# Two-layer transformer stack on one core: routed experts on gathered row blocks instead of on all rows

## The reference

```python
x = x + attn_a(layernorm(x))      # 16 heads of width 8 over 256 positions, relative position bias
x = x + ffn(layernorm(x))
x = x + attn_b(layernorm(x))      # attends over the 32 batch entries, for each of 256 positions and 16 heads
x = x + ffn(layernorm(x))

# ffn: one shared expert for every row, and the best 2 of 7 routed experts
out = expert(x, sg, su, sd)                       # silu(x @ g.T) * (x @ u.T), then @ d.T, inner width 352
probs = softmax(x @ wr.T + rb);  scores, idx = top_k(probs, 2);  scores /= scores.sum()
out += sum over e of w[:, e] * expert(x, rg[e], ru[e], rd[e])     # w is 0 but for the two chosen
```

## Time and profile before

| | before |
|---|---|
| median of three runs | 3308.56 us |
| span of the profiled execution | 3301.8 us |
| TensorE busy | 3036.2 us, 92% |
| VectorE busy | 2308.3 us, 70% |
| ScalarE busy | 1813.0 us, 55% |
| GpSimd busy | 1737.1 us, 53% |
| mean granted TensorE clock | 0.928 |
| moved by transfers | 139.94 MB, 42 GB/s |

### The profile page before, as it was taken

One profiled execution on the slowest core, in us unless ns is written; L12 is line 12 of the kernel. 1 busy time (PEld: TensorE's weight loads), 2 busy tenths in 40 slices (PEclk: granted clock), 3 DMA queues, 4 the chain that ended last, 5 costly groups with the idle time before them and its releaser, 6 DMA issues.

```text
span 3301.8 us, 87667 instructions
## 1 busy us (share of the span) xinstructions
PE 3036.2 (92%) x29986; PEld 2069.9 (63%) x29986; DVE 2308.3 (70%) x6980; ACT 1813.0 (55%) x3489; POOL 1737.1 (53%) x1382
## 2 busy tenths in 40 slices
PE   7899999999999999999999789999999999999998
PEld 4567666666666666666666456666666666666665
DVE  4568776767787677767767656766767667676667
ACT  5568666756676677667765334443434444444443
POOL 4145445544544464446444336665656666666664
PEclk7799999989999999999989779998989999998999
DMA  3011111111111111111111111111111111111111
GB/s 112 20 33 42 36 36 33 40 35 33 39 39 33 36 36 39 36 33 36 41 31 36 43 34 47 50 47 44 49 45 47 44 50 50 47 50 47 50 47 49
DMA packets 105967, 139.94 MB, mean 42 GB/s; under 512 B 13121, under 2 KB 51265, under 8 KB 105585
## 3 DMA queue, kind: packets, MB, share of 16 engines
q1 hardware_dynamic: 87408, 126.18, 12.8%
q10 hardware_dynamic: 18176, 8.92, 1.1%
HBM read 126.11 MB, written 8.95 MB: 41 GB/s over the span
## 4 chain that ended last, share of the span: by engine, by line
PE 81%; DVE 8%; issue 5%; ACT 1%; DMA 1%; POOL 1%; ACTq 0%; DVEq 0%; SPq 0%; POOLq 0%
PE bank_E L1236 13%; PE bank_E L1238 9%; PE bank_E L1237 9%; PE bank_T L1166 7%; PE bank_Y L1236 6%; PE bank_S L1157 6%; PE bank_Y L1238 4%; PE bank_Y L1237 4%; PE bank_O L1177 4%; PE bank_S L1129 3%; PE bank_O L1218 3%; PE bank_S L1138 3%; PE bank_S L1139 2%; PE bank_S L1201 1%; DVE xn L909 1%
## 5 line engine op out<-in xcount | busy, mean ns | idle before, releaser
L593 POOL TENSOR_TENSOR hid_lo<-work,hid_hi 128x512 fp32r<-128x512 f32 x660 | 841.1, 1287 | 766.4 <-ACT hid_hi L836 757.2
L725 POOL TENSOR_TENSOR work<-work 128x512 f32<-128x512 f32 x640 | 827.6, 1300 | 482.2 <-DVE work L1075 362.2
L829 ACT ACTIVATE work<-bank_E 128x512 f32<-128x512 f32 x704 | 420.1, 597 | 466.7 <-PE bank_E L1238 462.0
L1075 DVE TENSOR_TENSOR work<-work,bank_E 128x512 f32<-128x512 f32 x704 | 479.8, 683 | 170.8 <-PE bank_E L1238 75.1
L836 ACT ACTIVATE hid_hi<-work 128x512 fp32r<-128x512 f32 x704 | 441.5, 630 | 282.1 <-POOL work L725 181.9
L1068 DVE SCALAR_TENSOR_TENSOR work<-work,bank_E 128x512 f32<-128x512 f32 x704 | 480.2, 682 | 148.0 <-ACT work L829 146.2
L981 DVE CUSTOM_DVE_ANT_0 z<-bank_S,big 128x256 f32<-128x256 f32 x1024 | 390.4, 421 | 200.7 <-PE bank_T L1166 147.5
L787 ACT ACTIVATE z<-z,nm 128x256 f32<-128x256 f32 x1024 | 457.4, 501 | 40.9 <-DVE nm L981 39.0
L583 ACT COPY probT<-bank_T 128x512 f32<-128x512 f32 x512 | 296.5, 579 | 105.2 <-PE bank_T L1166 102.4
L1236 PE MATMUL bank_Y<-hid_hi,wd_hi 128*128 128x512 f32 x704 | 327.7, 465 | 24.8 <-POOL hid_lo L593 19.5
L1236 PE MATMUL bank_E<-xh,wu_hi 128*128 128x512 f32 x704 | 330.1, 469 | 1.0 <-DVE work L1068 0.8
(11 more groups left out here) (125 smaller groups left out, 4345.9 us busy)
## 6 DMA issues: line engine op xcount, KB each, us to landing
work<-wts_dram SPq DMA_DIRECT2D x224, 256.0 KB, 3.2
work<-wts_dram SPq DMA_DIRECT2D x128, 192.0 KB, 2.7
work<-wts_dram SPq DMA_DIRECT2D x128, 128.0 KB, 2.8
work<-wts_dram SPq DMA_DIRECT2D x128, 64.0 KB, 2.5
xin<-in_x SPq DMA_DIRECT2D x16, 256.0 KB, 2.8
x<-work ACTq DMA_DIRECT2D x16, 256.0 KB, 2.5
xin<-x SPq DMA_DIRECT2D x64, 64.0 KB, 1.9
out_x<-work ACTq DMA_DIRECT2D x64, 64.0 KB, 1.7
```

What stands on the lines that cost most here:

```text
L593: eng.tensor_tensor(hid_lo[:, n % CUT_RING, :], hid[:, n % H_RING, :], hid_hi[:, n % CUT_RING, :].bitcast(F32), ALU.subtract).then_inc(hl_ ...
L725: pool.tensor_tensor(h, h, weight[:, k % WB_RING, :], ALU.mult).then_inc(weighed, 1)
L829: act.activation(th[:, n % 2, :], product_bank(2 * n)[:, :], ACT.Tanh, scale=0.5).then_inc(th_ready, 1)
L1075: dve.tensor_tensor(hid[:, n % H_RING, :], th[:, n % 2, :], product_bank(2 * n + 1)[:, :], ALU.mult).then_inc(h_ready, 1)
```

## The change

The program is rewritten around the same mathematics:

- The passes keep the shared expert alone: 3 tiles (128, 128 and 96 columns). Its gate and up products keep three fp32r matmuls, its down product is one plain f32 matmul a tile, and the low part for it goes.
- A pass ranks its rows by chosen expert (two triangular products, "rank") and scatters each row twice, with its weight and its row number, into the region of its expert in memory (sent), by eight indexed transfers of 128 rows from GpSimd ("scat").
- After all 16 passes of a half, VectorE makes a table of which block of 512 rows belongs to which expert; 38 blocks (BLOCKS) are always run. SP reads the table, pads the regions, and fetches rows (six ahead) and weights (three ahead). A block is transposed, goes through its expert's three tiles, is transposed back and weighted, and GpSimd adds its rows into x2 or x3 by four indexed adding transfers, each block's after those of the block before have landed.
- The routed weights are cut into high and low parts once at the start and kept in memory (w_split).
- In A the selector matmuls go: 32 transfers a pass lay q and k out. In B 16 transfers put k of each head into a zeroed tile kw, and the scores are matmuls over 128 rows and 512 columns in four column tiles; the transposes are made on TensorE, and v is laid out by position so that the product with it is 16 matmuls of 36 columns for each quarter of a pass.
- The planner now lays out all 16 passes of a half at once, two passes ahead with the load and one with the projections, with new costs; there is no loop in the code any more. Rings are deeper (z 6, probT 8), and bank T is two banks. Stores go from the ACT queue to SP's; half B ends in x3 and is copied to the output.

The core of the diff:

```diff
-Z_RING = 4
-PT_RING = 5
+BLOCKS = 2 * ROWS // CHUNK + ROUTED - 1
+Z_RING, NM_RING, PT_RING = 6, 8, 8
+ZB_RING, PB_RING = 4, 2
+ROW_RING, WEIGHT_RING = 6, 3
...
+                        for k in range(4):
+                            src = (qk_hi, qk_lo)[(k // 2, k % 2)[n]][32 * j:32 * j + 32, n, :]
+                            dst = qx[32 * j + 8 * k:32 * j + 8 * k + 8, s, n, :, :]
+                            sp.dma_start(dst, src).then_inc(spread_landed[2 * s + n], 16)
...
+                    for h in range(HEADS):
+                        sp.dma_start(kw[8 * h:8 * h + 8, h, :], k_b[8 * h:8 * h + 8, :]).then_inc(kw_landed, 16)
...
+            def pad(half):
+                sp.wait_ge(table_ready, half + 1)
+                for e in range(ROUTED):
+                    r = sp.value_load(table[0:1, 2 * BLOCKS + e:2 * BLOCKS + e + 1], min_val=0,
+                                      max_val=EXPERTS * CAP - CHUNK)
+                    sp.dma_start(sent[bass.ds(r, CHUNK), :].rearrange("(t p) c -> p t c", p=P), padding[:, :, :]
+                                 ).then_inc(padded, 16)
...
+                    for k in range(2):
+                        for t in range(TOK):
+                            pool.indirect_dma_start(
+                                out=sent[:, :], out_offset=bass.IndirectOffsetOnAxis(
+                                    ap=target[:, s, k, t:t + 1].bitcast(U32), axis=0),
+                                in_=xs[:, s, k, t, :], in_offset=None).then_inc(sent_out[s], 16)
...
+                for b in range(half * BLOCKS, (half + 1) * BLOCKS):
+                    pool.wait_ge(emptied["T1"], use("E", b, "back"))
+                    after(pool, added, 64 * b)
+                    for t in range(TOK):
+                        pool.indirect_dma_start(
+                            out=dst[:, :], out_offset=bass.IndirectOffsetOnAxis(
+                                ap=xr[:, b % ROW_RING, t, D + 1:RW].bitcast(U32), axis=0),
+                            in_=yo[:, b % 2, t, :], in_offset=None, compute_op=ALU.add).then_inc(added, 16)
...
+            pool.memset(kw, 0.0).then_inc(kw_ready, 1)
...
+                    for j in range(4):
+                        lo = n * P + 32 * j
+                        last = pe.matmul(bank[name][32 * j:32 * j + 32, :], q_b[:, p % 2, lo:lo + 32],
+                                         kw[:, :, lo:lo + 32], start=True, stop=True, tile_position=(0, 32 * j))
...
+                    last = pe.matmul(bank["Y"][:, :], shared_d[0:size, n, :], hid[0:size, n, :], start=n == 0, stop=n == NT - 1)
...
+            def blocks(half):
+                first, last = half * BLOCKS, (half + 1) * BLOCKS
+                block_turn(first)
+                for b in range(first, last):
+                    block_products(b, 0)
+                    if b > first:
+                        block_down(b - 1, 2)
+                    if b + 1 < last:
+                        block_turn(b + 1)
+                    block_products(b, 1)
+                    block_down(b, 0)
+                    if b > first:
+                        block_back(b - 1)
+                    block_products(b, 2)
+                    block_down(b, 1)
+                block_down(last - 1, 2)
+                block_back(last - 1)
...
+            run("pe", "A", head, attention, tail)
+            blocks(0)
+            run("pe", "B", head, attention, tail)
+            blocks(1)
```

More of the change, by code:

```diff
@@ L121, in weight_loads @@
[L121 to L144, removed]
-WORK = {
[L149 to L156, removed]
-    "logits": {"pe": 1.6, "dve": 0.3}, "route": {"dve": 0.6, "act": 0.1},
-    "wturn": {"pe": 0.5, "dve": 0.6, "act": 0.1, "sync": 4.0}, "gate": {"pe": 0.65, "act": 0.5, "dve": 0.6},
-    "up": {"pe": 0.65, "dve": 0.6}, "weigh": {"pool": 1.25}, "cut": {"act": 0.55, "pool": 1.25, "dve": 0.6},
-    "down": {"pe": 0.65}, "sum": {"act": 0.5}, "end": {"pe": 0.5, "dve": 0.6, "act": 0.1},
-}
@@ new lines, in attention_uses @@
+def attention_uses(kind, p):
+    if kind == "A":
+        out = [(f"S{u % 2}", p, "scores", u) for u in range(UNITS)] + [(f"T{u % 2}", p, "probs", u) for u in range(UNITS)]
+        for n in range(MIXES):
+            out += [("O", p, "mix", n), ("O", p, "context", n)]
+        return out
+    out = [(f"S{t % 2}", p, "scores", t) for t in range(TOK)] + [(f"T{t % 2}", p, "probs", t) for t in range(TOK)]
+    return out + [("O", p, "mix", t) for t in range(TOK)] + [("O", p, "bturn", 0), ("O", p, "bout", 0)]
@@ new lines, with emptier @@
+LISTS = bank_uses()
+PLACE = {key: (name, k) for name, keys in LISTS.items() for k, key in enumerate(keys)}
+EMPTIES = {
+    "A": {"turn1": "act", "q": "act", "k": "act", "v": "dve", "scores": "dve", "probs": "act", "mix": "dve",
+          "context": "dve", "turn2": "act", "logits": "dve", "rank": "dve", "down": "act", "end": "dve",
+          "gate": "dve", "up": "dve"},
+}
+EMPTIES["B"] = EMPTIES["A"] | {"bturn": "act", "bout": "dve"}
+def emptier(kind, p, step, n):
+    if step == "down":
+        return ("act", p, "sum", 0)
+    return (EMPTIES[kind][step], p, step, n)
@@ L295, in steps_experts @@
[L295 to L313 removed]
+            return free_bank(kind, p, step, n)
@@ L314, in takes_part @@
+        return [("pe", p, "end", 0), ("sync", p - 2, "store", 0)]
+    if step == "store":
+        return [("dve", p, "end", 0)]
+HEAD_STEPS = ("load", "keep", "norm1", "turn1", "q", "k", "cut", "spr", "v")
+ATTENTION_STEPS = ("flip", "scores", "probs", "mix", "context", "bturn", "bout")
+def takes_part(kind, eng, step, n):
+    if eng not in WORK[kind][step]:
         return False
-    if eng == "act" and step == "route":
+    if step == "route" and eng == "act":
         return n == 1
-    if step == "weigh":
-        return n >= SHARED_TILES
@@ new lines, in passing @@
+    def passing(w, t):
+        if w[0] == "sync" and w[2] in ("load", "spr", "store"):
+            return LANDING
+        return HAND_OVER if w[0] != t[0] else 0.05
+    left, tail, ready = {t: len(u) for t, u in users.items()}, {}, []
+    ready = [t for t, n in left.items() if n == 0]
+    while ready:
+        t = ready.pop()
+        tail[t] = work(t) + max([passing(t, u) + tail[u] for u in users[t]], default=0.0)
+        for w in needs[t]:
+            left[w] -= 1
+            if left[w] == 0:
+                ready.append(w)
@@ L884, in settle, with then, normalise @@
                 dve.wait_ge(vstep, steps[0])
-            def normalise(p, rows, dst, k, done, n):
+            def then(instruction):
+                mark(instruction)
+                settle()
+            def normalise(src, dst, k, done, n):
                 v, y, a, b = (rs[:, k, m, :] for m in range(4))
```

1798 lines of the change are left out of this document (1026 added, 772 removed).

## The result

The changed kernel takes 2935.5 us (median of 4 runs, 2918.0 to 2936.0) against 3308.6 (4 runs, 3286.5 to 3311.7): ratio 0.887, interval 0.883 to 0.892. The forecast was 2780, in a range of 2440 to 3200. The profiled execution spans 2933.9 us, 162 more than the forecast's 2772.

The account below looks back on a forecast made before the run. TensorE was taken to set the pace, busy 92% of the span. A passes 16 x 72 = 1152, B 16 x 42 = 672, blocks 752 and seams 196 gave 2772 us of span, median 2780, range 2440 to 3200.

Parts of the forecast that it names:

- Faster, and inside the range: Whole kernel: faster by over 1% at chance 0.86, forecast 2780 us, range 2440 to 3200.
- Both hide: Spreading transfers: 15 us of SP's 72 in A, 10 of 42 in B, hidden; uncovered, 10 us a pass.
- rival for orders from untested costs: Planner's orders: passes waiting on bank Y's chain, 87 and 60 us, bring it to about 3307; chance 0.04.
- The clock step: TensorE's clock in A: 0.76, interpolated by share of 512-column products, so 55 us of work make a 72 us pass.
- the rule that I set against my own: TensorE's clock: throttled by default, released by activity; read as busy means full speed, a 62 us A pass.
- What an A pass needs: Work of one A pass at full clock: TensorE 55 us, VectorE 54, ScalarE 49.
- rival 1: TensorE holds full clock: passes of 62 and 37 us, blocks 8.9, total 2447; chance 0.25.
- B 42: B pass: TensorE 30 us, VectorE 33; at clock 0.76 TensorE needs 40, with waits 42, between 36 and 50.
- Blocks 9.9: 76 expert blocks: TensorE's 8.7 us at 0.88 of full pace, 9.9 each, bounds 8.7 and 11.4, 752 in all.
- rival 3: Blocks: GpSimd's adds at 3.76 us an issue make 17.5 us a block, total 3357, 1.5% slower; chance 0.10.
- the Trainium skill's lock between VectorE and GpSimd: Blocks: VectorE operations can lock GpSimd out of writing transfer descriptors, which would stretch the add issues; no size given.
- Seams: Start, tails, tables, fetches, drains, B's preparation and final copy outside the steady passes and blocks: 196 us.

Follow-up runs that it names:

- a3: Changed kernel with only two planner prices altered: a spread's issue on SyncE 11.5 us (was 1.2) in A, 10.7 (was 1.0) in B; 2637.7 us, ratio 0.797.
- b1: a3 plus the next pass's head ahead of the last pass's tail in the banks' order, in A and B; 2496.2 us, ratio 0.754.
- a4: Changed kernel with two of a block's four indexed adds left out, so sums are short, no candidate; 2797.6 us, ratio 0.845.
- a1: Changed kernel with k's sixteen layout transfers of an A pass issued by GpSimd, q's left on SyncE; 2918.2 us, ratio 0.881.
- b2: a3 plus k's sixteen transfers of an A pass issued by GpSimd, planned at 8.7 us; 2696.9 us, ratio 0.814.
- c4: c1 with each of the 32 spreading transfers of an A pass split in two of half the rows; 2759.5 us, ratio 0.835.
- c1: a3 plus the next pass's head ahead of the last pass's tail in the banks' order, in A alone; 2508.1 us, ratio 0.759.
- b3: a3 plus measured planner costs of the unit steps and scatters in the A passes; 2835.9 us, ratio 0.856.

## Why the prediction came out as it did

**Faster, and inside the range: right.** The work that leaves TensorE is what paid (busy 3036 us before, 2049 after). The range was wide, and part of the nearness is luck: two of the three main terms, B and the blocks, came out right for other reasons than mine.

**"Both hide": wrong, and the step that cost most.** I reckoned the issue at SP's 0.46 us from loads, 15 us, and compared it with the length of a pass. Three things were off. An issue of such a transfer is 0.71 us, so 22.7 us. The transfers themselves need about 25 us, whoever issues them, a term that I had for B (2 to 3 us to land) but not for A. And the cover of a spread is not the pass, it is what TensorE's fixed order puts between the cut and the first scores: 7.6 us in one pass and nothing in the next. That order was made for a spread of 2.4 us. I had a rival for orders from untested costs, at 0.04, but tied it to bank Y; the step to take was to set each new planned cost beside the time that I had myself worked out (2.4 against 15). a3 shows it by the two prices alone. I had put an uncovered spread at 10 us a pass; in A, TensorE stood still for 27.

**The clock step: right number, wrong mechanism.** I interpolated 0.76 by the share of 512-column products and got 55 / 0.76 = 72. The row at 552 to 590 us has 8.6 of its 37.6 busy us in such products, about the share of a new A pass, and 0.98; b1's A stretch has 0.95 at 94% busy. The changed kernel also runs the attention units of its first passes with no product of the experts and no other product of 512 columns beside them, the very work that I held to be slow, and has full clock; so had the kernel before, just behind the slow stretch:
```profile
80.00:130.00 50.00, 49.67 (x407) 32.78 (x406) 39.38 (x206) 49.71 (x116) 9.29 (x12) 1.00 0.28 90
```
```profile
75.00:84.00 9.00, 7.47 (x53) 4.67 (x52) 5.83 (x30) 7.88 (x19) 0.00 (x0) 1.00 0.01 3
```
So the mix of products does not set the clock. The mean of 0.78 is made of stalls at half clock, of the work right behind them, also at half (618 to 635 us), and of work at full clock. (The two shares were also counted unlike: the 17% have q and k in them, the 44% leave out q, k and the selector matmuls.) By the rule that I set against my own (the Trainium skill, TensorE: Matmul & The Clock Gate, The HAM clock gate: throttled by default, released by activity) the A stretch should run at full speed when it does not stall, and here the trace agrees (0.98 from 552 to 590 us), but for the first 17 us of work after a stall. Why the kernel before had 0.50 from 53 to 73 us at 99% busy remains open.

**What an A pass needs: nearly right.** I had 55 us of TensorE, 54 of VectorE, 49 of ScalarE; b1, with little waiting, takes 56.9 with TensorE busy 94% of it (53.5 us), VectorE 48.8, ScalarE 47.8. Only VectorE was 5 too high. That is the passes of rival 1 (62), even a little below. The forecast of 72 was too high for the kernel without the stall and too low with it.

**B 42: right number, other reason.** TensorE is busy 30.5 us a pass (305 in ten), but at a mean clock of 0.85, and my 30 were for full clock, so its work was put too high and the clock too low. The other 12 us are waits: in the ten passes 35 us for the transfers of k (16 issues of 0.67 us, 10.7 against my 7.4, and their landing) and 33 for VectorE's copies of v, and many small ones. The true price takes 3.7 us off a pass.

**Blocks 9.9: right number, wrong engine.** TensorE's share is 7.7 us, and 8.1 with its waits (a4), below my lower bound of 8.7: a group of three products takes 0.70 to 0.78 us there, not 0.81, and a set of transposes 0.36, not 0.55; the f32 product, put at 0.9, takes 0.86. It was divided by a guessed 0.88 of full pace, and that the result equals GpSimd's period is luck. GpSimd's chain, put at 4 x 1.1 + 2.5 = 6.9, comes to 9.65, and 9.9 measured from block to block: the mis-sized term is the issue, 1.56 us and 0.30 to the next, 1.86 for 1.1. It is the mechanism of rival 3 at half its price, so it made the block 1.8 us longer and not 7. As for the Trainium skill's lock between VectorE and GpSimd (SBUF — State Buffer, SBUF: two separate sides): the issues of a block are 1.55 to 1.61 us each while VectorE is busy 185 of 340 us, so no run here shows a stretched one.

**Seams** were 19 us short in the tables and fetches, 5 too long in the final copy. The first scores start at 72.2 us and not at 42 "as now", since nothing covers the first spread; these 30 us are part of A's 169. The splitting of the weights, put under 60 us, ends at 105.5; it cost nothing until a1 and b2 put k's spread behind it.

## What to carry to other kernels

Where a program orders its engines from a table of costs, compare every new entry with the time that you work out for that step: two entries ten times too small cost 298 us here. Ask of a hidden transfer how much work the consumer's fixed order puts between its start and its first reader, and count both its issue and its transfer time. A better table does not promise a better order, though: measured prices for the units made it 198 and 338 us worse, so each such change has to be timed. And before a queue gets new work, look at what stands in it at the start: it cost 41 and 45 us here.

## What the hardware showed that I had not expected

- A transfer from SBUF to SBUF of 64 KB in 32 rows takes SP 0.71 us to issue (0.68 in halves, 43.3 by 64), GpSimd 0.54 (8.71 by 16), against 0.46 for loads; while 32 of them run, 74 to 101 GB/s are moved (588 to 611 us in the changed kernel, 603 to 614 in a1), where the start of the kernel before moved 208 GB/s in its transfers from 42 to 53 us.
- The same bytes in halves kept the transfer engines less busy: share 0.20 at 61 GB/s from 604 to 647 us in c4, 0.49 at 81 GB/s from 606 to 630 in c1. Cause open, and so is what holds the rate of a spread at 80 GB/s or so: no run changed its layout alone.
- An indexed add of 128 rows costs GpSimd 1.56 us, an indexed copy of as many rows 0.98, each with 0.30 to the next; the adds that wait for a block's landing start 2.4 us after its last issue has ended.
- A stall costs twice: behind one of 23 us TensorE was granted 0.50 for 17 us more, at 97% busy (618 to 635 us in the changed kernel).
- Small changes of price move an A pass between 57 and 81 us with the same work in it. From a3 to b3, 9.4 of the 13.9 us are TensorE busy longer at a lower clock.
